# Output projection of an attention block: from eight straight groups to a seven-product scheme with operands in a ring

## What is computed

```
q, k, v = rope(c @ wq), rope(c @ wk), c @ wv            # c: the first layer's output
out     = softmax(q k^T / sqrt(128), causal) v          # 32 heads x 128 = 4096 columns
x1      = x + out @ wo                                  # wo: 4096 x 1024, the stage that is changed
result  = x1 + ffn(cond2(x1))
```

## Time and profile before

| | us |
|---|---|
| median of 3 runs (2760.72 to 2767.38) | 2761.23 |
| profiled execution, time | 2761.87 |
| profiled execution, span | 2759.7 |
| PE busy, of the span | 2693.2 (98%) |
| DVE / ACT / POOL busy | 1595.8 / 853.4 / 1010.0 |
| attention pairs of the first half | about 286 to 872 |
| output projection of the first half | 872 to 1235 |

### The profile page before, as it was taken

The page is one execution under the profiler, slowest core; times in us unless marked ns, Lnnn a source line. Parts: engine busy times, 40 slices in busy tenths (PEclk is TensorE's granted clock), DMA queues, the critical chain, the costliest instruction groups (busy, mean ns, idle before and its releaser), DMA issues.

```text
span 2759.7 us, 40669 instructions
## 1 busy us (share of the span) xinstructions
PE 2693.2 (98%) x13432; PEld 2223.4 (81%) x13432; DVE 1595.8 (58%) x2355; ACT 853.4 (31%) x2039; POOL 1010.0 (37%) x678
## 2 busy tenths in 40 slices
PE   8989899999999999999998989999999999999999
PEld 7868788888887888877887878888888788887887
DVE  2124566666777666665525356666667765666452
ACT  2223344444443212121203334444444321122120
POOL 0030766666663222220303076666666222221020
...
GB/s 213 212 209 72 73 66 74 77 77 78 71 60 145 123 80 110 91 54 56 113 134 147 46 73 77 78 77 72 68 77 77 143 110 92 98 106 39 84 92 71
DMA packets 281654, 263.15 MB, mean 95 GB/s; under 512 B 67834, under 2 KB 217466, under 8 KB 281474
## 3 DMA queue, kind: packets, MB, share of 16 engines
...
...
## 4 chain that ended last, share of the span: by engine, by line
PE 89%; issue 3%; SPq 2%; DVE 2%; POOL 2%; DMA 1%; ACT 1%; DVEq 0%; ACTq 0%; POOLq 0%
PE prod L742 27%; PE prod L744 26%; PE prod L743 26%; PE turned L934 4%; PE turned L959 2%; PE turned L946 1%; PE turned L736 1%; POOL slot_f L1658 1%; POOL slot L1663 1%; SPq L551 1%; SPq L526 1%; PE prod L1160 0%; PE turned L924 0%; DMA raw<-in_wv 0%; PE prod L788 0%
## 5 line engine op out<-in xcount | busy, mean ns | idle before, releaser
L2088 DVE TENSOR_TENSOR x<-prod,x 128x512 f32<-128x512 f32 x512 | 347.2, 689 | 265.5 <-PE prod L744 264.9
L1706 POOL TENSOR_TENSOR w_lo<-raw,w_hi 128x1024 fp32r<-128x1024 f32 x64 | 157.0, 2454 | 578.6 <-ACT w_hi L1462 578.6
L742 PE MATMUL prod<-c_hi,w_hi 128*128 128x512 f32 (+1 forms) x832 | 328.6, 395 | 9.3 <-DVE q_rot L2003 5.9
L744 PE MATMUL prod<-c_hi,w_lo 128*128 128x512 f32 (+1 forms) x832 | 325.0, 391 | 0.0
L743 PE MATMUL prod<-c_lo,w_hi 128*128 128x512 f32 (+1 forms) x832 | 324.7, 390 | 0.0
L742 PE MATMUL prod<-c_hi,slot 128*128 128x512 f32 x768 | 309.4, 403 | 15.7 <-ACT p_sum L1382 12.6
L744 PE MATMUL prod<-c_hi,slot 128*128 128x512 f32 x768 | 301.4, 392 | 0.0
L743 PE MATMUL prod<-c_lo,slot 128*128 128x512 f32 x768 | 300.9, 392 | 0.0
L1997 DVE TENSOR_TENSOR rope_sin<-prod,consts_sb 64x512 f32<-64x512 f32 x320 | 220.3, 688 | 97.0 <-PE prod L744 84.2
L742 PE MATMUL prod<-x_hi,w_hi 128*128 128x512 f32 x656 | 261.4, 398 | 9.1 <-DVE h_masked L1846 3.8
L744 PE MATMUL prod<-x_hi,w_lo 128*128 128x512 f32 x656 | 257.2, 392 | 0.0
...
## 6 DMA issues: line engine op xcount, KB each, us to landing
o_scratch<-o_f ACTq DMA_DIRECT2D x64, 512.0 KB, 3.1
raw<-in_wo SPq DMA_DIRECT2D x64, 512.0 KB, 3.3
raw<-t_scratch SPq DMA_DIRECT2D x34, 512.0 KB, 3.5
raw_a<-in_wq SPq DMA_DIRECT2D x32, 512.0 KB, 5.0
raw<-in_wq SPq DMA_DIRECT2D x32, 512.0 KB, 4.8
c_lo_f<-o_scratch SPq DMA_DIRECT2D x32, 512.0 KB, 4.9
o_xf<-o_scratch SPq DMA_DIRECT2D x32, 512.0 KB, 5.3
t_scratch<-x ACTq DMA_DIRECT2D x17, 512.0 KB, 4.8
```

The lines of the kernel that those rows point to most:

```text
L742: pe.matmul(dst, wh, xh, start=start, stop=False, skip_group_check=skip)
L744: return pe.matmul(dst, wl, xh, start=False, stop=stop, skip_group_check=skip)
L1706: pool.tensor_tensor(WL[j % 2][:], RAW[j % 2][:], WH[j % 2][:].bitcast(F32), ALU.subtract).then_inc(split_d, 1)
L2088: dve.tensor_tensor(X1[:, xs], PJ[q % 4][:], X1[:, xs], ALU.add).then_inc(taken, 1)
```

## The change

The output projection becomes a sequence of 19 slots, written out without a loop, each a 2x2 block product in the seven-product form that the attention stage uses, with its own names for the semaphores (`b_prod`, `b_whi`, `b_wlo` and so on). The inner dimension is cut into 16 sub-blocks u (a pair of heads each), and the output into four pairs of row blocks, r and r + 4. Slot s works on row pair (s + 1) % 4 and on sub-blocks s - 3 to s, which lie in a ring of four columns in the buffers of `c` and its sums (`part`, `part(n)[.][:, u % 4]`). So slots 3 to 15 have four k-tiles (7 x 4 x 3 = 84 matmuls), slots 0, 1, 2 and 16, 17, 18 have 1, 2, 3 and 3, 2, 1; 64 k-tiles x 21 = 1344 matmuls a half.

- The seven operands of each sub-block are not the heads but blocks and sums of them. `o_store` writes units 0 and 1 of a block (three of its four pieces plain: the second unit stores one piece, the first two), POOL forms four sums of a block in place (`parts`), ACT stores them (`parts_store`, 1 MB). In the attention stage this stands in POOL's `weights` between the low part of P2 and the sum for P5, for two pairs of three, and the last two blocks in slots 1 and 4.
- SP loads seven operands of 256 KB a slot (`load_part`), each once PE has finished with the column's old content, and the weights in pieces with rows of 128 columns (`load_b_raw`), for slot s + 2 once POOL has finished slot s.
- ACT makes seven high parts of weights (`w_hi_b`) and seven of the heads (`o_hi`) a slot, in the order of `STEPS`; its copy of P1 is `p1_copy_b`.
- POOL makes five sums and seven low parts a slot (`weights_b`), in slots 0 and 1 also the low parts of the heads. From slot 2 on these are VectorE's (`o_lo`, seven a slot).
- VectorE adds results into x1 with eight operations a slot (`add`, and one into a bank) instead of 32 a group. x1's rows are loaded one or a few at a time into space that the attention stage leaves (`X1O`, x_row in the listing), slot 0's as soon as `comb` is through, and are copied back to their place by ACT, eight copies of 128x1024, ahead of the router's exponential. `m_take` waits for these copies (`x1_cp`).

The core of the diff:

```diff
+def k_tiles(s):
+    return max(0, s - SUBS + 1), min(4, s + 1)
+def row_of(s):
+    return (s + 1) % 4
...
+        def part(n):
+            def grid(j, t):
+                return [view(w[:], KC)[:, j:j + 4, t * NT:(t + 1) * NT] for w in (CH, CL, CLF)]
+            return {P1: lambda: grid(0, 0), P2: lambda: grid(4, 0), P3: lambda: grid(4, 1), P7: lambda: grid(0, 1),
+                    P4: lambda: [view(w[:], 4) for w in (T4H, T4L, T4LF)],
+                    P5: lambda: [view(w[:], 4) for w in (T1H, T1L, T1LF)],
+                    P6: lambda: [view(w[:], 4) for w in (T2H, T2L, T2LF)]}[n]()
...
+                    for h in range(2):
+                        c = (row_of(s) + 4 * h) * P
+                        dst = RAWA[2 * (s % 2) + h][:].rearrange("p (j k n) -> p j k n", j=2, k=4)
+                        for k0, k1, u in segments(s):
+                            for j in range(2):
+                                sp.dma_start(dst[:, j, k0:k1], wo_v[:, j, u:u + k1 - k0, c:c + P]
+                                             ).then_inc(b_raw[s % 2], 16)
...
+                def load_part(u, n):
+                    if u == 0:
+                        sp.wait_ge(a_prod, hf * A_STEP["a_prod"] + (NP * (PAIRS - 1) + n + 1))
+                    elif u >= 4:
+                        sp.wait_ge(b_prod, hf * (NP * SLOTS_B) + (NP * (u - 1) + n + 1))
...
+                TAIL = {(0, P1): [(turn_p, 5)], (0, P6): [(pv, 5), (score, 6)], (0, P7): [(score, 7)],
+                        (1, P2): [(turn_p, 6)], (1, P5): [(pv, 6)], (1, P4): [(turn_p, 7)], (2, P6): [(pv, 7)]}
...
+                def slot(s):
+                    k0, k1 = k_tiles(s)
+                    new = s % 4 if s < SUBS else None
+                    ks = [k for k in range(k0, k1) if k != new] + ([new] if new is not None else [])
+                    for n in OPS:
+                        for f, u in TAIL.get((s, n), ()):
+                            f(B, u)
+                        pe.wait_ge(b_wlo, hf * WLO_HALF + wlo_count(s, n))
+                        if n == P2:
+                            pe.wait_ge(b_p1, hf * SLOTS_B + (s + 1))
+                        elif n in (P7, P3):
+                            pe.wait_ge(x1_step, xb + (X_OPS * s + {P7: X12A, P3: X22A}[n]))
+                        elif s == 0:
+                            pe.wait_ge(qk_in, hf * A_STEP["qk"]
+                                       + qk_count(PAIRS - 1, {P1: R11, P6: R22, P5: R12, P4: R21}[n]))
+                        else:
+                            pe.wait_ge(x1_step, xb + (X_OPS * (s - 1) + {P1: X11, P6: X21A, P5: X12, P4: X21}[n]))
+                        for i, k in enumerate(ks):
+                            if k == new:
+                                if s < POOL_O:
+                                    pe.wait_ge(b_olo_p, hf * (NP * POOL_O) + (NP * s + n + 1))
+                                else:
+                                    pe.wait_ge(b_olo_v, hf * (NP * (SUBS - POOL_O)) + (NP * (s - POOL_O) + n + 1))
+                                hold(pe)
+                            hi, lo, _ = part(n)
+                            ws = slice(k * P, (k + 1) * P)
+                            mm = three(PJ[BANK[n]][:], slot_hi(n)[:, ws], slot_lo(n)[:, ws], hi[:, k], lo[:, k],
+                                       n in OPENS and i == 0, i == len(ks) - 1, skip=True)
+                        mm.then_inc(b_prod, 1)
+                for s in range(SLOTS_B):
+                    slot(s)
                 x_base = pe.snap(hf * (TT * KC))
...
+                def parts_store(B, b):
+                    act.wait_ge(part_in, B["part"] + (4 * b + 4))
+                    act.dma_start(o_d[bass.ds(B["row"] + (NP * b + 2), 4)].rearrange("h p n -> p h n"), view(OF[:], 4)
+                                  ).then_inc(parts_out, 16)
...
+                def o_hi(u, n):
+                    act.wait_ge(o_in[n][u % 2], hf * (16 * SUBS // 2) + 16 * (u // 2 + 1))
+                    hi, _, f = part(n)
+                    act.copy(hi[:, u % 4], f[:, u % 4]).then_inc(b_ohi, 1)
...
+                    act.copy(P1S[:], PJ[BANK[P1]][:]).then_inc(b_p1, 1)
...
+                TAIL = {(0, 0): [(take_p, 5)], (0, 2): [(o_store, 5)], (0, 5): [(exp, 6)], (0, 9): [(exp, 7)],
+                        (1, 3): [(take_p, 6)], (1, 5): [(parts_store, 2)], (1, 6): [(o_store, 6)],
+                        (1, 9): [(take_p, 7)], (2, 3): [(o_store, 7)], (3, 9): [(parts_store, 3)]}
+                STEPS = [("p1", 0, 0), ("o", 0, P4), ("w", 1, P1), ("w", 1, P6), ("o", 0, P3), ("w", 1, P2),
+                         ("o", 1, P1), ("w", 1, P5), ("o", 1, P6), ("w", 1, P7), ("o", 1, P2), ("w", 1, P4),
+                         ("o", 1, P5), ("w", 1, P3), ("o", 1, P7)]
...
+                    b11, b21, b12, b22 = (OF[:, i * NT:(i + 1) * NT] for i in range(4))
+                    n = n_part + 4 * b
+                    pool.tensor_tensor(b11, b12, b11, ALU.subtract).then_inc(part_in, 1)
+                    pool.tensor_tensor(b12, b22, b12, ALU.subtract).then_inc(part_in, 1)
+                    pool.wait_ge(part_in, n + 1)
+                    pool.tensor_tensor(b22, b22, b11, ALU.subtract).then_inc(part_in, 1)
+                    pool.wait_ge(part_in, n + 3)
+                    pool.tensor_tensor(b21, b22, b21, ALU.subtract).then_inc(part_in, 1)
...
+                    if lp >= 4 and (lp - 1) % 3 != Q23:
+                        parts(2 * ((lp - 3) // 3) + ((lp - 1) % 3 == Q01), B["stored"], B["part"])
...
-                with pool.Fori(0, NKV) as g:
-                    dg = pool.snap(hf * SPLIT_D + g * PER_G)
-                    for j in range(PER_G):
-                        pool.wait_ge(wd_hi, dg + (j + 1))
-                        hold(pool)
-                        pool.tensor_tensor(WL[j % 2][:], RAW[j % 2][:], WH[j % 2][:].bitcast(F32), ALU.subtract
-                                           ).then_inc(split_d, 1)
...
+                    add(s2, a21, a11, ALU.subtract)
+                    pool.wait_ge(b_sum, hf * (5 * SLOTS_B) + (5 * s + 1))
+                    add(s2, s2, a22, ALU.add)
+                    if 1 <= s <= POOL_O:
+                        o_lo(s - 1, P3)
+                    if s < POOL_W:
+                        lo(P1, a11)
+                    lo(P6, s2)
+                    if s < POOL_W:
+                        lo(P2, a12)
+                    if s == 1:
+                        o_lo(1, P1)
+                        parts(2, B["stored"], B["part"])
+                    if s == 0:
+                        o_lo(0, P1)
+                    if s == 4:
+                        parts(3, B["stored"], B["part"])
+                    add(f32(P5), a21, a22, ALU.add, P5)
+                    lo(P5, f32(P5))
+                    if s == 0:
+                        o_lo(0, P6, P2)
+                    if s == 1:
+                        o_lo(1, P6)
+                    add(f32(P7), a11, a21, ALU.subtract, P7)
+                    lo(P7, f32(P7))
+                    if s == 1:
+                        o_lo(1, P2)
+                    if s < POOL_O:
+                        o_lo(s, P5)
+                    if s < POOL_W:
+                        lo(P4, a22)
+                    add(f32(P3), a12, s2, ALU.subtract, P3)
+                    lo(P3, f32(P3))
+                    if s < POOL_O:
+                        o_lo(s, P7, P4)
+                for s in range(SLOTS_B):
+                    weights_b(s)
...
-                        dve.tensor_tensor(X1[:, xs], PJ[q % 4][:], X1[:, xs], ALU.add).then_inc(taken, 1)
...
+                    o_lo(s, P4)
+                    formed(P6)
+                    dve.wait_ge(b_p1, hf * SLOTS_B + (s + 1))
+                    dve.tensor_tensor(bank[P6], P1S[:], bank[P6], ALU.add).then_inc(x1_step, 1)
+                    if s < 4:
+                        for h in range(2):
+                            dve.wait_ge(x_in[row_of(s) + 4 * h], hf * 32 + 32)
+                        hold(dve)
+                    stepped(U2B)
+                    add(x12, bank[P6])
+                    o_lo(s, P3)
+                    if s == 0:
+                        before_exp(B, 6)
+                    formed(P2)
+                    add(x11, bank[P2])
+                    if s == 1:
+                        normalise(B, 7)
+                    o_lo(s + 1, P1)
+                    formed(P5)
+                    add(x22, bank[P5])
+                    o_lo(s + 1, P6)
+                    if s == 0:
+                        before_exp(B, 7)
+                        normalise(B, 6)
+                    formed(P7)
+                    stepped(X22A)
+                    add(x22, bank[P7])
+                    add(x21, bank[P7])
+                    o_lo(s + 1, P2)
+                    if s >= SUBS:
+                        x_lo_of(s - 1)
+                    formed(P4)
+                    stepped(X21A)
+                    add(x21, bank[P4], ALU.subtract)
```

(7 more changed lines are left out.)

474 lines of the change are left out of this document (249 added, 225 removed).

## The result

The changed kernel takes **2787.14 us** (median of 4 runs, 2786.58 to 2788.32), beside 2761.99 of the kernel before: ratio 1.0088, 95% interval 1.0070 to 1.0105. The profiled execution took 2786.79 us with a span of 2784.7, against 2761.87 before: 24.9 us more, where the forecast said 12.2.

A forecast was written before the change was run, and what follows sets the result against it. The prediction took PE, busy 98% of the span, as the bound. Against 2761.87 us it summed -87.1 (matmuls) + 26.8 (steady slots) + 67.5 (head) + 3 (tail) + 2 (attention stage) = +12.2, 2774 us, range 2728 to 2798.

The forecast's parts named there:

- case 4: The forecast's own case for the whole kernel: gain and losses nearly cancel, 2757 to 2790 us; chance 0.54.
- the landing of x1's rows: Head, slot 0: rows 1 and 5 land 3.1 to 7.7 us after issue, taken as 5.5.
- POOL's slot: Steady slots: 17.26 us plus seven collisions with VectorE's low parts at 0.43 makes 20.27, 1.22 over PE's 19.05.
- head, slots 0 to 4: Start of each half's projection: PE waits 41.2 us on a chain through POOL, 7.4 there before; +33.8 a half, +67.5.
- steady slots 5 to 15: Eleven projection slots a half: PE waits for POOL's longer slot, 13.4 us a half, +26.8 in all.
- tail, beyond before's wait of 1.7: Short slots 17 and 18, where POOL needs longer than PE: 1.5 us a half, +3 (0 to 6).
- attention stage: POOL's four parts in two of three pairs and their store, barely hidden: +2 us in all (0 to 24).
- The clock in the head: Head: after PE's pauses of over 3 us the granted clock restarts low, adding 2 us.
- the cushion: Weight slots: PE trails POOL by most of a slot, but ACT's P1 copy leaves 13.6 us of products behind POOL's last sum.
- 1 (low parts in POOL's waits): Steady slots: VectorE's low parts fall into POOL's three waits, PE stays the bound, 2727 us; chance 0.25.
- 2 (a head under 25 us): Head: links through row 1, mask and exponential do not close; 20 us less a half, 2734 us; chance 0.08.
- 3 (the attention stage): take_p or o_store late by 1.5 us in 16 pairs, and rows land at 7.7: 2802 us; chance 0.13.

The follow-up runs named there:

- rows_first: Changed kernel with the loads of x1's rows 1 and 5 moved ahead of sub-block 1's seven parts on SP's queue: 2780.88 us.
- mask_first: Changed kernel with mask, row maximum and scale of attention unit 6 put on VectorE ahead of the add waiting for x1's rows: 2777.88 us.
- zero_3: Changed kernel with VectorE's low parts of the attention output for P6, P5 and P7 set to zero from sub-block 2 on: 2751.17 us.
- zero_7: Changed kernel with all seven of VectorE's low parts of the attention output set to zero from sub-block 2 on: 2740.66 us.
- po_first: Changed kernel with P1's copy and the attention output's high parts for P7 and P4 ahead of the next slot's P3 weight cast on ACT: 2768.06 us.
- p1_first: Changed kernel with only the copy of P1's bank moved ahead of the next slot's P3 weight cast on ACT: 2786.05 us.

## Why the prediction came out as it did

The sign was right, though the prediction itself called it weak, and the mechanisms were those of its case 4; its size, +12.2 us, was half of the measured +24.9. The step that failed is the sum of the head: its first link, the landing of x1's rows, was put at 5.5 us and took 8.56. POOL's slot, put at 20.27 us, was the second, at 20.69. By its own steps, for one half (first half's trace):

| step | forecast | measured |
|---|---|---|
| matmuls | -43.6 | -43.6 |
| head, slots 0 to 4 | +33.8 | +38.6 |
| steady slots 5 to 15 | +13.4 | +15.6 |
| tail, beyond before's wait of 1.7 | +1.5 | +2.0 |
| attention stage | +1 | +0.6 (0.9 in the second half) |

The first matmul of slot 5 starts at 990.34, 120.5 us into the stretch; without waits it would be 946.4 - 871.85 = 74.6, and 7.4 of waits were there before. Slot 15 ends at 1201.97 + 13.6 = 1215.6, so eleven slots took 225.2, less 209.6 for their matmuls. From there to 1247.90 are 32.3 us, less 28.6 for the 126 matmuls of the tail and before's 1.7. Without the attention stage the measured column sums to 12.6; the stretch grew by 12.5.

- **Mis-sized: the landing of x1's rows.** "to landing 3.1 to 7.7 us, I take 5.5". It took 8.56. The row at 7.7 was the same transfer, x1's, and 5.5 was the middle of two rows, not the nearest one. The kernel was also to issue eight parts (2 MB) right ahead of it, and in the trace 381 GB/s move there: the rows stood in a queue. The rows were also issued 4.8 us into the stretch and not 4.0. From this link on all comes late: the cast of P2 for slot 1 ends at 18.64 us instead of 15.15, 3.5 of the head's 4.8. rows_first and mask_first show the link by two ways, and rows_first that less ahead of the rows lands them sooner (6.30).
- **Mis-sized: POOL's slot.** 17.26 + 7 x 0.43 = 20.27 was forecast, 20.69 measured. The seven collisions all come, at 0.44 by zero_3, so the error is small there (0.1). The larger part, 0.3 to 0.4, is the base: a free slot is 17.67 by zero_3, and the steps between POOL's starts in zero_7, where nothing collides, add up to 17.7 as well once its waits for PE are taken out. Three of them, from a sum to its low part with the wait for ACT's cast between, are 2.10 each where the pair of the earlier trace rows has 2.03, 1.99 and 1.98; they hold 0.3 of the difference. Why they are longer stays open. Over eleven slots it is 4.6 us a half, of which 2.2 show in the steady row: PE ended slot 4 late, with 2.6 us lost to the lower clock in P2, so that in slot 5 it had nothing to wait for. In slots 2 to 4 POOL was 1.2 us longer than forecast and in slot 1 shorter by 0.7, so the cast's 3.5 us had become 4.0 at POOL's last sum of slot 4. (The line through the earlier trace rows gives 0.71 and 1.00 us for 256 and 384 columns, and not 0.73 and 0.98; 0.73 and 1.01 were measured. It changes nothing.)
- **The clock in the head:** +2 was forecast; P2 of slot 4 alone took 5.3 us (974.04 to 979.33) for twelve matmuls worth 2.7. Ahead of it the lower clock costs PE too, but PE would wait for POOL's chain in that time anyway: up to slot 5, PE is idle for 30.3 us, not the 35 to 45 that the prediction named as a sign, and most of the rest of the 46 us beyond its work (38.6 and the 7.4 of before) is work at the lower clock (0.84 granted in the mean).
- **Right:** the matmuls' cost, so that a pitch of 19.05 shows as soon as POOL's hold is gone; that all seven low parts collide, and by ACT's order (po_first changes the order, and five collide in full); the wait of 1.2 us on p_sum in each slot (1.3 measured); the gap on the mask in slot 0 (7.1 for 5); no wait for SP's loads in the slots.
- **Incomplete: the cushion.** ACT's copy was named as what ties PE to POOL's last sum. It is one of two; p1_first gained 1 us, po_first 19, most of it by POOL's shorter slots.

Of the rivals, 1 (low parts in POOL's waits) is excluded by the seven long operations, 2 (a head under 25 us) by 38.6, 3 (the attention stage) by the 0.6 to 0.9 us and by PE never waiting on probs_t there, though its second part, rows that land at 7.7, was nearer to the truth than my own value. Head and steady slots are 2 x (4.8 + 2.2) = 14 us over their forecast, and the tail 1; the attention stage is 0.5 under its own, the second half's stretch grew by 0.6 less than the first's, and the stages that the change does not touch gave back 1 us. That is the miss of 12.7, to 0.2.
